# Last passes of an autocorrelation in an order of their own, and a Sinkhorn chain begun one pass earlier

## The reference

```python
# autocorrelation, per head, over the 128 tokens
corr = ifft(fft(q) * conj(fft(k))).real
w, idx = top_k(corr, 9); w = softmax(w)
out = sum(w[i] * take(v, minimum(idx[i] + pos, L - 1)) for i in range(9))
# mixing
logits = x_norm @ W.T + base          # 16 for H_res, 4 for H_pre, 4 for H_post
H_res = sinkhorn_log(H_res_logits)    # 50 iterations on a 4x4 matrix per token
y = einsum(x_streams, softmax(H_pre)) @ W_branch
x = x + einsum((1 - g) * I + g * H_res, x_streams) + einsum(y, softmax(H_post))
```

## Time and profile before

| what | us |
|---|---|
| median of 3 runs (1228.21 to 1229.78) | 1228.88 |
| the profiled execution | 1230.26 |
| its span, from the first to the last instruction | 1228.4 |

### The profile page before, as it was taken

One profiled execution on the slowest core, in us unless ns is written; L12 is line 12 of the kernel. 1 busy time (PEld: TensorE's weight loads), 2 busy tenths in 40 slices (PEclk: granted clock), 3 DMA queues, 4 the chain that ended last, 5 costly groups with the idle time before them and its releaser, 6 DMA issues. The chain is left out here.

```text
span 1228.4 us, 23475 instructions
## 1 busy us (share of the span) xinstructions
PE 1022.5 (83%) x7936; PEld 776.0 (63%) x7936; DVE 929.4 (76%) x2818; ACT 610.1 (50%) x1803; POOL 486.6 (40%) x676
## 2 busy tenths in 40 slices
PE   5699999999999999999657999999898787615056
PEld 4577777877777777777445677777666564313034
DVE  6766786666787666776604878879999999997994
ACT  6434555444555544555515667777565564212023
POOL 2523433333443333443313766666565563101020
PEclk9799999999999999999778999999999998857579
DMA  9011011111011111011122222422332211139025
GB/s 378 29 42 51 25 58 58 58 47 51 17 58 58 58 58 41 28 47 42 47 100 86 86 91 74 129 91 78 91 106 74 75 56 39 43 116 343 0 52 137
DMA packets 47234, 95.71 MB, mean 78 GB/s; under 512 B 5952, under 2 KB 30400, under 8 KB 47168
## 3 DMA queue, kind: packets, MB, share of 16 engines
q1 hardware_dynamic: 47168, 94.91, 23.1%
HBM read 64.48 MB, written 27.26 MB: 75 GB/s over the span
## 5 line engine op out<-in xcount | busy, mean ns | idle before, releaser
L614 POOL TENSOR_TENSOR prob_G<-prob_G,rl 128x512 f32<-128x512 f32 x96 | 100.0, 1042 | 257.3 <-DVE rl L502 257.3
L384 ACT ACTIVATE prob_G<-prob_G,negm 128x128 f32<-128x128 f32 x384 | 148.9, 390 | 88.8 <-DVE negm L444 88.8
L244 PE MATMUL ps_qkv<-w_hi,xT_hi 128*128 128x512 f32 x384 | 156.6, 408 | 12.5 <-DVE prob_G L507 8.5
L245 PE MATMUL ps_qkv<-w_lo,xT_hi 128*128 128x512 f32 x384 | 151.6, 395 | 0.0
L246 PE MATMUL ps_qkv<-w_hi,xT_lo 128*128 128x512 f32 x384 | 151.2, 394 | 0.0
L316 PE MATMUL ps_qkv<-wo_hi,aT_hi 128*128 128x512 f32 x256 | 108.0, 422 | 0.0
L318 PE MATMUL ps_qkv<-wo_hi,aT_lo 128*128 128x512 f32 x256 | 102.3, 399 | 0.0
L317 PE MATMUL ps_qkv<-wo_lo,aT_hi 128*128 128x512 f32 x256 | 102.1, 399 | 0.0
L244 PEld LDWEIGHTS ps_qkv<-w_hi,xT_hi 128*128 128x128 f32 x384 | 73.1, 190 | 39.0 <-issue 17.0
L440 DVE TENSOR_TENSOR prob_G<-ps_s,mask 128x512 f32<-128x512 f32 x96 | 64.9, 676 | 41.0 <-PE ps_s L227 40.5
L469 DVE TENSOR_TENSOR xT_lo<-ps_t,xT_hi 128x512 fp32r<-128x512 f32 x16 | 11.1, 691 | 102.9 <-ACT xT_hi L423 102.9
(11 more groups left out here) (248 smaller groups left out, 2773.0 us busy)
## 6 DMA issues: line engine op xcount, KB each, us to landing
xin<-in_x SPq DMA_DIRECT2D x16, 512.0 KB, 3.3
xres<-in_x SPq DMA_DIRECT2D x16, 512.0 KB, 5.2
x<-xres SPq DMA_DIRECT2D x16, 512.0 KB, 2.6
c_xin<-x SPq DMA_DIRECT2D x16, 512.0 KB, 5.2
c_cin<-in_ctx SPq DMA_DIRECT2D x16, 512.0 KB, 4.5
c_b_xres<-x SPq DMA_DIRECT2D x16, 512.0 KB, 3.3
rows_x<-c_row SPq DMA_DIRECT2D x64, 128.0 KB, 2.3
m_xm<-rows_x SPq DMA_DIRECT2D x16, 512.0 KB, 8.6
```

The source lines that it names most:

```text
L244: nc.tensor.matmul(ps_qkv[:, n, :], xT_hi[:, k, :], w_hi[:, k, cols], start=k == 0, stop=False)
L245: nc.tensor.matmul(ps_qkv[:, n, :], xT_hi[:, k, :], w_lo[:, k, cols], start=False, stop=False)
L384: r = nc.scalar.activation(prob(g)[:, j, :], prob(g)[:, j, :], ACT.Exp, bias=negm[:, h:h + 1], accum_out=lsum[:, h:h + 1])
L614: nc.gpsimd.tensor_tensor(prob(g), prob(g), rl[:, g * GROUP:(g + 1) * GROUP].rearrange("p (j o) -> p j o", o=1).to_broadcast([P, GROUP, T] ...
```

## The change

It does four things. The first steps of a chain are issued within one period, with a logarithm between each (`begun_in`, new parts 5, 6 and 7 of a pass), and chain a gets forty steps already in pass 7, so that it stands at 306 by the end of pass 14, and chain b at 14. TensorE, ScalarE and VectorE leave the passes 15 to 17 to functions of their own (`ending`); GpSimd and SyncE keep theirs. In these the weights' products are made and transformed in halves, chain b is issued by counts (`fill`), and b and c together in the end (`both`), so that b stands at 76 and c at 30 when the phase ends. In pass 14 the weights are scaled by eight instructions on VectorE, and not by one on GpSimd, and transposed as they come. In the mixing, ScalarE issues chain b's logarithms of the first block ahead of the copies and rows of chain a, and chain c's of the second block after row 9, and not after row 11. One semaphore for three steps (`h_step`) becomes three (`lg_done`, `hx_done`, `hr_done`).

```diff
...
-        steps_to = {(6, 0): ((one_a, 2),), (6, 2): ((one_a, 3),), (6, 4): ((one_a, 6),),
-                    (7, 1): ((one_a, 7),), (7, 2): ((one_a, 8),)}
-        at = 8
-        for b in range(8, B - 1):
-            if b == 11:
+        steps_to, logs_at = {}, {}
+
+        def begun_in(b, chain):
+
+            for part, to in ((0, 2), (1, 3), (5, 6), (2, 7), (3, 8)):
+                steps_to[b, part] = ((chain, to),)
+            for k, part in enumerate((5, 6, 1, 7, 2)):
+                logs_at[b, part] = ((chain, k + 1),)
+
+        begun_in(6, one_a)
+        steps_to[6, 4] = ((one_a, 10),)
+        at = 10
+        for b in range(7, B - 2):
+            if b == 10:
                 parts = {0: at + 3, 1: at + 9, 2: END[0], 3: END[1], 4: END[1] + 10}
+                logs_at[b, 2] = ((one_a, 6), (one_a, 7), (one_a, 8))
             else:
                 parts = {0: at + 3, 1: at + 9, 2: at + 29, 4: at + 40}
             for part, to in parts.items():
                 steps_to[b, part] = ((one_a, to),)
             at = parts[4]
-        steps_to[14, 0] += ((one_b, 2),)
-        steps_to[14, 2] += ((one_b, 3),)
-        steps_to[14, 4] += ((one_b, 6),)
-        steps_to.update({(15, 0): ((one_b, 8), (one_a, END[2])), (15, 1): ((one_b, 22),), (15, 2): ((one_a, END[3]), (one_b, 46)), (15, 3): ((one_b, 50),),
-                         (15, 4): ((one_b, 56),), (16, 0): ((one_b, 88),), (16, 3): ((one_c, 2),), (16, 4): ((one_b, 100), (one_c, 6)),
-                         (17, 0): ((one_b, 116),), (17, 4): ((one_b, 126), (one_c, 16))})
-        logs_at = {(6, 1): ((one_a, 1),), (6, 2): ((one_a, 2),), (7, 0): ((one_a, 3),), (7, 1): ((one_a, 4),), (7, 2): ((one_a, 5),),
-                   (11, 2): ((one_a, 6), (one_a, 7), (one_a, 8)),
-                   (14, 1): ((one_b, 1),), (14, 2): ((one_b, 2),), (15, 0): ((one_b, 3), (one_b, 4), (one_b, 5)),
-                   (15, 1): ((one_a, 9), (one_a, 10)), (15, 2): ((one_a, 11),),
-                   (16, 2): ((one_c, 1), (one_c, 2)), (17, 2): ((one_c, 3), (one_c, 4), (one_c, 5))}
+        begun_in(B - 2, one_b)
+        steps_to[B - 2, 0] += ((one_a, at + 3),)
+        steps_to[B - 2, 1] += ((one_a, at + 9),)
+        steps_to[B - 2, 2] += ((one_a, END[2]),)
+        steps_to[B - 2, 4] = ((one_b, 14),)
+        logs_at[B - 2, 2] += ((one_a, 9), (one_a, 10))
...
+            if ending is not None:
+                ending()
+                return
...
+            def ending():
+
+                n = LAST
+                for i in range(KD):
+                    pe.wait_ge(w_done, n + i + 1)
+                    if i == 0:
+                        pe.wait_ge(lg_done, n - 1)
+                    r = nc.tensor.transpose(f_d[:, i * T:(i + 1) * T], wgt[:, i, :], idf[:])
+                    if i % 4 == 3:
...
+                pe.wait_ge(x2_done, 2 * n)
+                pe.wait_ge(v_done, 2 * n + 2)
+                weight_spectrum(p_b, 0)
+                branch_transposed(n - 2)
+                weight_spectrum(p_c, 1)
+                branch(n - 2)
+                out_half(0)
+                out_half(1)
+                pe.wait_ge(y_done, n - 1)
+                row_transposed(n - 1)
+                row_logits(n - 1)
+                pe.wait_ge(lg_done, n)
+                row_transposed(n)
+                row_logits(n)
+                branch_transposed(n - 1)
+                pe.wait_ge(lg_done, n + 1)
+                branch(n - 1)
+                branch_transposed(n)
+                pe.wait_ge(y_done, n)
+                branch(n)
+
             pe.wait_ge(fwd_in, 16)
-            iterations(pe, body)
+            iterations(pe, body, ending)
...
-                chain_logs(b, 0)
...
+                def shares(m):
+                    act.wait_ge(hx_done, m + 1)
+                    act.wait_ge(hr_done, m)
+                    act.wait_ge(xp_step, XS * m)
...
+                for h in range(2):
+                    act.wait_ge(wT_ps, n + h + 1)
+                    nc.scalar.activation(wT[:, h * HALF:(h + 1) * HALF], p_d[:, h, :], ACT.Copy).then_inc(wT_done, 1)
+                normalised_row(n - 1)
+                branch_copy(n - 2)
+                branch_out(n - 2)
+                log(one_a, FIRST_LOGS + 2 * BLOCK_LOGS, FIRST_LOGS + 2 * BLOCK_LOGS)
+                act.wait_ge(x2_bias_done, n + 1)
+                nc.scalar.activation(squares[:], x2[:], ACT.Square, bias=x2_bias[:], scale=1.0 / D ** 0.5,
+                                     accum_out=x2_var[:]).then_inc(x2_sq_done, 1)
+                row_turned(n - 1)
+                normalised_row(n)
+                row_turned(n)
+                shares(n - 1)
+                log(one_c, 1, FIRST_LOGS)
+                branch_copy(n - 1)
+                branch_out(n - 1)
+                shares(n)
+                branch_copy(n)
+                branch_out(n)
+
+            iterations(act, body, ending)
...
+                up_to(b, 5)
...
+                    if isinstance(b, int) and c == LAST:
+                        dve.wait_ge(wrec_done, c + 1)
+                        for i in range(KD):
+                            nc.vector.tensor_scalar(wgt[:, i, :], wgt[:, i, :], wrec[:, i:i + 1], None, ALU.mult).then_inc(w_done, 1)
...
+                def fill(count):
+                    advance(dve, one_b, one_b.issued + count)
+
+                def both(count):
+                    weave(dve, (one_b, one_b.issued + count), (one_c, one_c.issued + count))
...
+                def branch_in(m):
+                    dve.wait_ge(he_done, 2 * m + 2)
+                    nc.vector.reciprocal(fact(m, m % 2, AT_HR, 2), hs[:]).then_inc(hr_done, 1)
+                    both(1)
+                    for i in range(1, NS):
+                        if i == 1:
+                            dve.wait_ge(xp0_done, m + 1)
+                        else:
+                            dve.wait_ge(xp_step, XS * m + i - 1)
+                        nc.vector.scalar_tensor_tensor(xp[:], row[m % 2][:, i * C:(i + 1) * C], he[:, i:i + 1], xp[:], ALU.mult, ALU.add).then_inc(xp_step, 1)
+                        both(1)
+
+                advance(dve, one_a, END[3])
+                fill(2)
+                dve.wait_ge(ws_ps, 2 * n + 1)
+                dve.wait_ge(v_done, 2 * n + 2)
+                dve.wait_ge(out_ps, 2 * n)
+                for h in range(2):
+                    product(tw_re, f_b, v_re, h)
+                    product(tw_im, f_b, v_im, h)
+                    fill(1)
+                dve.wait_ge(ws_ps, 2 * n + 2)
+                for h in range(2):
+                    product(tw_re2, f_c, v_im, h)
+                    product(tw_im2, f_c, v_re, h, -1.0)
+                    fill(1)
+                dve.wait_ge(xres_in, 16 * (n + 1))
+                dve.wait_ge(x3_done, n)
+                residual(0)
+                fill(6)
+                residual(1)
+                fill(14)
+                gate_logits(n - 1)
+                gate_max(n - 1)
+                fill(6)
+                gate_logits(n)
+                dve.wait_ge(lg_done, n + 1)
+                weave(dve, (one_c, FIRST), (one_b, one_b.issued + FIRST))
+                branch_in(n - 1)
+                gate_max(n)
+                both(4)
+                branch_in(n)
+                both(10)
+
+            iterations(dve, body, ending)
...
-                if near:
+                if near and not (isinstance(b, int) and c == LAST):
...
+            logs(one_b, FIRST_LOGS + 1, FIRST_LOGS + BLOCK_LOGS)
             copies(one_a)
-            take_out(0, 2)
-            logs(one_b, FIRST_LOGS + 1, FIRST_LOGS + BLOCK_LOGS)
-            take_out(2, one_a.n)
+            take_out(0, one_a.n)
             logs(one_c, FIRST_LOGS + 1, FIRST_LOGS + BLOCK_LOGS)
             logs(one_b, FIRST_LOGS + BLOCK_LOGS + 1, FIRST_LOGS + 2 * BLOCK_LOGS)
             copies(one_b)
-            take_out(one_b.first_row, LAST - 1)
+            take_out(one_b.first_row, LAST - 3)
             logs(one_c, FIRST_LOGS + BLOCK_LOGS + 1, FIRST_LOGS + 2 * BLOCK_LOGS)
-            take_out(LAST - 1, LAST)
+            take_out(LAST - 3, LAST)
             copies(one_c)
             take_out(LAST, B)
```

More of the change, by code:

```diff
@@ L1001, in out_half @@
                 def out_half(n):
-                    if not near:
-                        for i, part in enumerate((tw_re, tw_im, tw_re2, tw_im2)):
-                            if n == 0:
-                                pe.wait_ge(tw_done, 4 * b + (2, 2, 3, 4)[i])
-                            r = nc.tensor.matmul(p_b[:, n, :], mats[:, INV_OUT + i % 2, :], part[:, n * HALF:(n + 1) * HALF],
-                                                 start=i == 0, stop=i == 3)
-                        r.then_inc(out_ps, 1)
-                        return
                     for i, part in enumerate((tw_re, tw_im)):
@@ L1102, in body, with weight_spectrum, branch_transposed, branch @@
                     out_half(1)
+            def ending():
```

(42 more changed lines are left out.)

81 lines of the change are left out of this document (65 added, 16 removed).

## The result

The changed kernel takes 1244.93 us (median of 4 runs, 1243.94 to 1246.02) where the kernel before takes 1228.99 beside it: a ratio of 1.0124, 95% interval 1.0111 to 1.0137, 15.9 us more. The forecast was 1234.5 us with a range up to 1240. The sign was right, the size was not: the time lies above the range. The profiled execution took 1244.16 us and has a span of 1242.1, 13.7 more than before.

A forecast was written before the change was run, and what follows sets the result against it. The end was taken to hang on when chain b is finished, plus 52.3 us. 1.8 - 10.7 + 14.8 - 0.2 = +5.7 us on the 1228.4 us span, adjusted to the median: 1234.5 us, range 1226 to 1240.

The forecast's parts named there:

- A: Passes 6 to 14, to pass 14's ninth value: +3.2 for pass 7's forty steps, -1.4 in pass 14, net +1.8 us.
- 4 if one more pass meets GpSimd badly: Upper bound given for stretch A, passes 6 to 14: +4 us in place of +1.8.
- B: From pass 14's ninth value to the first mixing step: 56.6 us instead of 67.25, so -10.7 us.
- the bound of 46.1: Length in us of stretch B if none of its four waits (1.3, 1.7, 2.7, 4.8) came.
- C: From the first mixing step to chain b's end: 18.1 - 8.7 + 1.7 + 3.7 = +14.8 us (11 to 17).
- The -8.7: In the mixing, VectorE's stall for chain b's logarithms goes, as they stand ahead of chain a's copies and rows: -8.7 us.
- D: The 52.3 us after chain b: chain c's 64 saved lone steps bring almost nothing, -0.2 us.
- rival 2: Compact ending, in B: TensorE at full clock, VectorE never waits, B 46.1, 10.5 us less: 1224 us; chance 0.18.
- Rival 4: TensorE at half clock from the spectrum to the output halves (+3.5) and A at 4: 1240 us and above; chance 0.07.

The follow-up runs named there:

- e6: Changed kernel with one step of chain a less beside the first residual of passes 8 and 13, issued at the pass's end instead: 1238.21 us, ratio 1.0055.
- e3: Changed kernel with five more matrix products, computing nothing new, on TensorE in its idle gap in each of passes 7 to 14: 1240.74 us, ratio 1.0082.
- e7: Changed kernel with e3's products from pass 8 on, e6's moved steps, e4's twelve steps and e5's order: 1230.07 us, ratio 0.9990.
- e8: Kernel before, with chain b's logarithms ahead of chain a's copies and rows, and chain a's step beside the first residual moved in passes 8 and 14: 1218.81 us.
- e5: Changed kernel with the old ScalarE order in the mixing, rows 0 and 1 taken out ahead of chain b's logarithms: 1240.94 us, ratio 1.0082.
- e4: Changed kernel with twelve more steps of chain b at the autocorrelation's end, where VectorE stood idle: 1237.17 us, ratio 1.0060.
- e9: Changed kernel with chain a's forty steps put back one pass, the last 19 in the ending, and pass 8's step beside the first residual moved: 1240.86 us.
- e10: e8 with five more products on TensorE in each of passes 8 to 14, ahead of the wait for the residual: 1220.07 us, ratio 0.9923.

## Why the prediction was wrong, and where it was right

**A, the failed step.** I wrote that pass 14 loses 2.6 us with its fourteen steps and gets 1.1 back for three lone ones, net -1.4. It became 1.62 us longer, an error of 3.0. The count was right: with the collision out of the way the pass takes 24.42 (e6). What failed is that nothing stood against the -1.4. The new numbering puts a chain step in GpSimd's way in this pass, which costs 1.3 us, and TensorE's clock falls, which costs 1.5 (both from e3, e6 and e7; what made it fall is open). What I missed was the place: the trace of before had shown me how a chain step fares beside GpSimd's scaling (1.49 us, the line at 1033.53 under e8), and I used it only to price GpSimd's removal in the ending. I never asked which step of the *new* numbering would stand there in the passes before. Starting the forty at 10 instead of 8 moved the hit from pass 14's tail, behind the ninth value, to pass 13's tail, where 1.2 us become 2.8. "4 if one more pass meets GpSimd badly" was in the text, as a bound; the kinds of step can be counted modulo six, so it should have been the forecast.

The rest of the error of 5.7: passes 8, 9 and 13 are 2.3 longer (+0.79, +0.81, +0.70), TensorE's clock by e3, which takes 2.8 off the three: the granted clock was 1.00, 0.94 and 1.00 before, 0.94, 0.88 and 0.94 after, and 1.00, 0.94 and 1.00 in e3. Why it fell more in the changed kernel is not shown. I took neighbouring passes to be unchanged, though the clock of 0.94 in some of them could be read before. Passes 6 and 7 are 4.2 longer, not 3.2. Passes 10 to 12, where the pass with a block's end now comes one earlier, give 0.6 back.

**B** came to 58.4 for 56.6. Step by step: the eight scalings take about 0.21 us each, where I had 0.18:

```profile
1041.34 1.26 DVE L1467 TENSOR_SCALAR c_wgt<-c_wgt,c_wrec 128x128 f32<-128x128 f32 x6
```

The wait for the spectrum is 1.2 (1.3 said), the idle end 4.4 (4.6 from 52.0 to 56.6, though the bound of 46.1 counts it as 4.8), the wait for the last shares 2.7 (2.7). The logits of row 15 were the error: I had them reach VectorE at 34.9 us after the ninth value, and they do at 36.9. TensorE does the logits of row 14 and of row 15 one after the other, each sixteen records at half clock:

```profile
1063.61 3.61 PE L1154 MATMUL pair<-c_w_sb,c_x3T 128*128 128x24 f32 x16 [2.80 <-ACT c_x3T L1314]
...
1070.21 3.61 PE L1154 MATMUL pair<-c_w_sb,c_x3T 128*128 128x24 f32 x16 [0.69 <-ACT c_x3T L1314]
```

I had counted one wait of 1.7; there are two, 1.63 and 4.13.

**C** is 94.7 for 95.5, with chain c's stall at 2.9 (2.7 to 4.7 said, 3.7 taken), and with one row at half clock where I had assumed two. e6 has two, and its stall is 5.0 (18.1 in all less the 13.1 behind chain b), 2 us more, as I had put on that row:

```profile
DVE chain_c_logm L684 <- ACT chain_c_lcb L721: 18.1, 2, 13.1
```

The -8.7 in this sum is right as a difference to before, but the reason given for it (the new order on ScalarE) is not: with the old order the wait doesn't come back (e5).

**D** is unchanged, and the other kernels confirm its rule: from the first instruction of chain b's coefficients to the end it takes 52.8 to 53.3 us in eight of the twelve traces and 54.5 to 55.0 in the four (e4, e7, e9, e10) where more of the rows behind it are mixed at half clock, whatever is done for chain c.

**The rivals.** The compact ending (rival 2) failed as said: the stage waits for its last stores, and e4 shows what VectorE could have done meanwhile. Rival 4 came nearest, 1240 and above with A at 4, though by another mechanism: half clock was not in the output halves but in the passes.

So the change trades 8.9 us of ending for 50 steps of chain b (18 us, of which the 8.7 of the old wait are to be taken off), brings chain a forward for about 2 us of profit, and loses that through one step more in GpSimd's way ahead of a ninth value and through TensorE's clock.

## What to carry to other kernels

A chain that sets the end should be followed step by step: shortening the code around it gives nothing unless the chain gets its steps in the time that falls free, and idle time of the engine that carries it at a stage's end is a gift (twelve steps of filling, 7.1 us at the end of the chain). When steps are renumbered, list which *kind* of step now falls beside each long instruction of an engine that it can collide with, in every period, since a hit ahead of a value that TensorE waits for cost up to twice its own length here, in pass 14 about half of it by the step and half by TensorE's clock. And an order in a queue is right only for the arrival times that it was made for: the same three logarithms, moved ahead, gained 5.7 us in one plan and lost 4.0 in the other, so each part of a compound change is worth trying alone.

## What the runs showed of the hardware

A VectorE product of two SBUF inputs of 128x80 lasts 1.49 us instead of 0.23 when it starts inside GpSimd's 1.90 us product, and ends with it; the reciprocal and the reduction beside it (0.27, 0.29), and a residual with one input in PSUM (0.69), don't change. The Trainium skill, page "SBUF — State Buffer", section "SBUF: two separate sides", describes an exclusive lock of a shared pair of ports, held for a whole instruction, in which a VectorE operation with two SBUF inputs takes part. The trace agrees, for the held step and for those with one input.

TensorE's granted clock is 0.87 over pass 14 in the changed kernel, with gaps of 2.02 and 0.92 us, and 1.00 in e6, with one of 1.99; records at the lower clock take 0.63 us instead of 0.39. The gap's length doesn't decide it: in e6 one gap of 2.01 in pass 9 and one of 2.59 in pass 12 are followed by a stretch at half clock (0.94 over the pass), where pass 12 of the changed kernel, with 2.60, stays at 1.00. Five products that nobody reads, put in the gap, keep pass 14 at 1.00 and take 1.5 us off it; pass 9, where the held step stands as well, stays at 0.94.
